# Attention block with 16 routed experts: GpSimd waits for a group's four scatters before the next group's

## The reference, cut to what matters

```python
x = x + attention(layernorm(x), ctx, ctx)            # 16384 tokens of 256 values; 16 heads of 16
xn = layernorm(x)
shared = (silu(xn @ sfc1.T) * (xn @ sfc2.T)) @ sfc3.T
top_w, top_idx = top_k(xn @ gate_w.T, 2)             # two of 16 experts for each token
w = softmax(top_w)
h = silu(einsum('td,ehd->teh', xn, w1))              # 16 experts, 256 -> 128
moe = einsum('teh,te,edh->td', h, dispatch(w), w2)   # 128 -> 256, weighted and summed
x = x + moe + shared
```

## Time and profile before

| | us |
|---|---|
| three runs | 1846.89, 1858.83, 1862.25 |
| median | 1858.83 |
| the profiled execution, its time | 1852.7 |
| its span | 1850.9 |

### The profile page before, as it was taken

How to read it: one execution, slowest core, us unless ns; L and a number is a source line. 1 busy time by engine, 2 the same in 40 slices (tenths; PEclk the granted TensorE clock), 3 DMA queues, 4 the chain that set the end, 5 groups by cost and what they waited for, 6 DMA issues and landing times.

```text
span 1850.9 us, 50328 instructions
## 1 busy us (share of the span) xinstructions
PE 1504.5 (81%) x17109; PEld 1318.8 (71%) x17110; DVE 1345.4 (73%) x3378; ACT 726.3 (39%) x1346; POOL 1234.2 (67%) x1109
## 2 busy tenths in 40 slices
PE   5599999999999999999999999875667676666674
PEld 4588787877787878777878788764656665566563
DVE  6588888888888888888888888863445455454453
ACT  3344444454444444544454445331222222222231
POOL 4387777777777777778777877765455554454455
PEclk9799999999999999999999999987788888888887
DMA  8788889878887988789878887747666675666573
GB/s 208 166 186 180 179 201 182 180 169 213 176 177 160 227 176 174 161 221 183 173 173 216 174 175 157 191 176 237 193 208 199 189 209 161 194 203 198 179 209 115
DMA packets 945833, 344.74 MB, mean 186 GB/s; under 512 B 824088, under 2 KB 898730, under 8 KB 940288
## 3 DMA queue, kind: packets, MB, share of 16 engines
q1 hardware_dynamic: 901680, 216.53, 56.9%
q0 software_dynamic: 33600, 92.91, 14.2%
q10 hardware_dynamic: 10512, 34.79, 5.8%
HBM read 200.37 MB, written 148.15 MB: 188 GB/s over the span
## 4 chain that ended last, share of the span: by engine, by line
PE 40%; DVE 18%; issue 16%; SPq 11%; POOL 5%; DMA 5%; ACT 4%; another core or an unknown queue 1%; DVEq 0%; POOLq 0%; ACTq 0%
SPq L337 4%; SPq L331 4%; PE bank_y L1145 3%; ACT xn L613 3%; PE bank_a L1158 3%; PE bank_y L1143 3%; PE bank_y L1144 3%; PE bank_a L1143 3%; DVE ln_stats L897 2%; PE bank_z L1143 2%; DVE ctx_lo L880 2%; PE bank_a L1297 2%; PE bank_a L1145 2%; PE bank_a L1144 2%; PE bank_u L1143 2%
## 5 line engine op out<-in xcount | busy, mean ns | idle before, releaser
L400 POOL DMA_INDIRECT slots<-xn,slot_i x256 | 281.6, 1100 | 96.0 <-issue 55.7
L517 POOL DMA_INDIRECT sums<-v_area,tail x144 | 144.0, 1000 | 144.4 <-DVE v_area L1096 98.8
L517 POOL DMA_INDIRECT out<-v_area,tail x144 | 143.6, 997 | 135.6 <-DVE v_area L1096 91.6
L1386 PE MATMUL bank_a<-ident,k_area 128*128 128x128 f32 x576 | 96.1, 321 | 140.8 <-DMA k_area<-slots 140.3
L1386 PEld LDWEIGHTS bank_a<-ident,k_area 128*128 128x128 f32 x576 | 77.8, 165 | 150.7 <-DMA k_area<-slots 150.1
L1096 DVE SCALAR_TENSOR_TENSOR v_area<-bank_y,tail,v_area 128x256 f32<-128x256 f32 x288 | 121.4, 478 | 68.4 <-remote 31.2
L690 ACT ACTIVATE th<-bank_z 128x512 f32<-128x512 f32 x72 | 43.0, 597 | 280.9 <-remote 135.6
L1075 DVE TENSOR_TENSOR xn_lo<-v_area,xn_hi 128x512 fp32r<-128x512 f32 x72 | 50.2, 698 | 140.2 <-ACT xn_hi L697 71.4
L409 POOL DMA_INDIRECT sums<-v_area,slot_i x128 | 128.1, 1001 | 33.2 <-issue 29.4
L1143 PE MATMUL bank_y<-wsh_out_hi,hid_hi 128*128 128x256 f32 x512 | 143.1, 279 | 1.3 <-POOL hid_lo L431 1.3
L1144 PE MATMUL bank_y<-wsh_out_lo,hid_hi 128*128 128x256 f32 x512 | 142.8, 279 | 0.0
(11 more groups left out here) (222 smaller groups left out, 5283.9 us busy)
## 6 DMA issues: line engine op xcount, KB each, us to landing
k_area<-slots SPq DMA_DIRECT2D x288, 129.0 KB
v_area<-sums SPq DMA_DIRECT2D x288, 128.0 KB
kv_dram<-w_sb SPq DMA_DIRECT2D x32, 1024.0 KB
x_sb<-in_x_in SPq DMA_DIRECT2D x32, 512.0 KB
ctx_sb<-in_ctx_t SPq DMA_DIRECT2D x32, 512.0 KB
q_dram<-q_sb SPq DMA_DIRECT2D x32, 512.0 KB
k_area<-kv_dram SPq DMA_DIRECT2D x256, 64.0 KB
w_sb<-q_dram SPq DMA_DIRECT2D x256, 64.0 KB
```

What stands on the lines that cost most here:

```text
L400: pool.indirect_dma_start(slots[j], bass.IndirectOffsetOnAxis(ap=slot_i[:, par, j, i:i + 1], axis=0), row_of[j][:, i, :], None).then_inc(S ...
L517: pool.indirect_dma_start(target, bass.IndirectOffsetOnAxis(ap=tail[:, r, t, 1 - j:2 - j].bitcast(u32), axis=0), y_ring[:, r, t, :], None, ...
L1386: last = nc.tensor.transpose(A[t // 2][:, t % 2 * C + k * P:t % 2 * C + (k + 1) * P], x_ring[:, r, t, CHANNEL[j] + k * P:CHANNEL[j] + (k + ...
```

## The change

After the four scatters of a quad, GpSimd waits until the semaphore of their ring place shows that all four have landed, and only then goes on to the next quad. `at(16, n - r, 64)` is 16(n-r)+64, the value that the semaphore has when this quad's four scatters, and all before them of the same place, are in. It holds for both choices, so 72 times.

```diff
@@ -516,6 +516,7 @@
                         pool.sem_inc(S["add_marked"], 1)
                     pool.indirect_dma_start(target, bass.IndirectOffsetOnAxis(ap=tail[:, r, t, 1 - j:2 - j].bitcast(u32), axis=0),
                                             y_ring[:, r, t, :], None, bounds_check=last, oob_is_err=False).then_inc(S[f"added{r}"], 16)
+                pool.wait_ge(S[f"added{r}"], at(16, n - r, 64))
```

## The result

The changed kernel takes 1895.4 us (1893.5 to 1897.7, four runs), the one before 1856.6 beside it: ratio 1.0215, 95% interval 1.0169 to 1.0262. It is slower by some 39 us; 1890 was predicted. The profiled execution took 1895.72 with a span of 1893.9, so 43.0 over the span before.

A forecast was written before the change was run, and what follows sets the result against it. The prediction took a three-quad loop of waits, 7.75 us a quad, to bound the kernel; POOL's one-quad loop +14, lost time +12, branch +8 and jitter +4 gave +38 on 1852.7, kept as 1890, range 1852 to 1925.

The forecast's parts named there:

- Pace: Experts' phase: POOL's new one-quad loop takes at least 7.95 us a quad against 7.75, +14 us over 71 steps.
- the branch: Every fourth wait stands before POOL's loop branch, hidden until now: 0.45 us each for 17 branches, +8 us.
- First to fourth start: POOL's issue of a quad's four scatters: 3.88 us from first start to fourth.
- Landing: From the fourth scatter's start to its landing: 3.2 us, as SP's x loads will be in flight.
- Restart: After a real wait POOL's sequencer no longer runs ahead: 0.87 us before the next scatter begins.
- Lost time is no longer made up: After late quads, POOL follows at 7.95 instead of 5.16: choices' turn 3.9, before quad 38 2.7, before 57 5.7; +12 us.
- Jitter: Small late loads in the experts' phase beyond the three-quad loop's slack: 0.05 us a quad, +4 us.
- the loop spans three quads: Kernel before, experts' phase: landing, SP's sums and x loads, transposes, product, DVE's sum, scatters set 7.75 us a quad.
- Rival A: POOL's holes absorb the wait, as the three-quad loop sets the pace: 0 to +18 us, about 1861; chance 0.18.
- Rival B: Waits space the quads evenly at 7.27 us if fourth start to landing is under 2.5: -22 us, 1831; chance 0.05.
- Rival C: SP's loads and POOL's scatters collide after each landing: 8.35 to 8.95 us a quad, about 1930; chance 0.15.
- Rival D: The semaphore's value is reached before the landing, so the wait isn't real and nothing changes; given no chance.

The follow-up runs named there:

- the short pause: Kernel before, no landing wait; after each quad POOL subtracts 8 columns of data nobody reads and waits for that: 1824.8 us, ratio 0.9815.
- the half hold: Kernel before, no landing wait; after each quad POOL subtracts 448 columns of data nobody reads and waits for that: 1847.7 us, ratio 0.994.

## Why the prediction was right, and where it wasn't

The direction, the size (+39 against +38) and the cause (POOL's own loop of one quad) were right. That the cause is POOL's time is shown from three sides: a hold of the same length without a landing gives the same pace (8.32), the wait placed where the landing is hidden costs nothing, and the changed kernel's time doesn't move when SP's order is turned (1898.8 against 1897.9; paces 8.34 and 8.24). But that the sum came so near was in part luck, as its errors cancelled:

- Pace, predicted 7.95, or 8.06 with the branch; measured 8.24. First to fourth start 4.07 for 3.88: 70 of the 288 issues took 1.06 to 1.5 instead of 0.98. Landing 3.13 for 3.2, right. Restart 0.97 on average for 0.87, and 1.24 over the branch, so the branch costs 0.27 for the 0.45 supposed. Worth 588.6 - 550.4 - 3.9 (the next term) = +34, where pace and branch were put at +22.
- "Lost time is no longer made up", +12: only the turn of the choices remained, 6.97 against 3.1, +3.9. The holes before quads 38 and 57 didn't come back. A long wait of ACT stands before each (9.60 and 11.23 us, ending at 1582.0 and 1732.7), and with the change's pauses of 3 us these waits are 5.4 at most. Jitter, +4: none to be seen.
- **The step that failed** is the first one, "the loop spans three quads" through the landing and SP's loads. SP's and PE's waits there had no price: with the landing taken out of SP's way the time stayed (0.9986). Nor do holes of 6 us follow each three quads "nearly throughout": the trace has 11 of over 5 us among 71 gaps, and they go with ACT's long waits. So on the slower chips the change can be read as two things: the pauses bring what the short pause brings alone, 33 us, and POOL's loop adds (8.24 - 7.28) x 71 = 68, 35 net; +30 was measured on that chip. That is a sum that fits, not a proof: the 33 come with fewer waits of ACT, but also with quads evenly spaced, and no run of the slower kind has one without the other.
- Rival A fell with the size of the loop, 8.24. Rival B had the pace right: evenly spaced quads do go at 7.28, 33 us faster, but with a pause of 1.2. Its condition was too wide: the half hold's gap of 2.1, as a landing of 2.2 would give, brought 10 us and not 22. (Of the twelve pieces two are under 2.5 and one is at it, where three or four were counted.) Rival C's collision doesn't show: the landings stayed at 3.13, and the slower issues (4.07) come as well with the hold that follows no landing (4.11). What slows them is open: of the 70 long ones 38 lie over one of DVE's copies of `w_sb`, of the other 218 only 51, and both DVE's copies and SP's x loads have their fixed place in the quad. Rival D: the wait is real.
- The range's low end, 1852, is called the middle of A but is its low end; the middle is 1861.
- The Trainium skill ("DMA: Bandwidth & Descriptors", the anatomy of a DMA on the GpSimd path) has a fixed 2.0 us plus bytes over 436 GB/s, by which 2.3 for the landing was an estimate. This trace doesn't agree: the mean of 70 is 3.13, and only six are under 2.5, among them 2.12 and 2.20 at the ends of the two choices, where SP's loads have run out.

## What to carry to other kernels

A wait for a DMA on the queue that issues the next ones turns a pipelined transfer into a serial one: issue + landing + restart must stay under the pace of the rest, or that engine is the bound. Placed where other issues cover the landing, it cost nothing here. And idle time that the profile can't name (remote) in a regular pattern deserves a look at all other engines at its end, before any loop is made responsible.

## What the runs showed of the hardware that I had not expected

- In 15 to 19 places of each of the five traces from the slower kind that have no pause after each quad, ACT's tanh waited over 5 us (mostly 9 to 10) while POOL scattered, and started, but for at most one a trace, 0.9 to 1.8 us after POOL paused. In about two thirds of them POOL's gaps were 0.3 us throughout, in the others some were 0.4 to 1.0. A pause of about 1.2 us between quads left none over 5 us. What holds ACT is open: its input was complete by the profile's modelled times, and no run separated a delayed signal from a delayed instruction.
- It isn't there on every chip. In the four traces from chips where the kernel before takes 1810 to 1812 tanh never waits for "remote", though one of them has 16 bursts of two whole quads; all ten from the slower kind have 10 to 29 such waits. No profile of the kernel before was taken on a quick chip, so that this makes the 50 us between the chips is argued, not shown.
- After a real wait POOL's next scatter starts 0.97 us after the landing (0.95 to 1.03, once 1.27), 1.24 when a loop's branch lies between.
